# A single 512-wide scan per state group, and the inverse root of the variance as a power on GpSimd

## The reference

```python
def step(s, rkvw):
    r_t, k_t, v_t, w_t = rkvw
    a = k_t[..., :, None] * v_t[..., None, :]
    out = jnp.einsum('bhi,bhij->bhj', r_t, u * a + s)
    s = a + w_t[..., :, None] * s
    return (s, out)
```

```python
m = x.mean(-1, keepdims=True)
v = ((x - m) ** 2).mean(-1, keepdims=True)
(x - m) / jnp.sqrt(v + eps) * w + b
```

## Time and profile before

| | |
|---|---|
| time, 3 runs | 1427.91 us median (1426.55 to 1428.36) |
| the profiled execution, its own time | 1426.46 us |
| its span, first to last instruction | 1424.7 us |
| TensorE busy | 1272.8 us (89%) |
| VectorE busy | 978.7 us (69%) |
| ScalarE busy | 581.5 us (41%) |
| GpSimd busy | 563.7 us (40%) |
| mean granted TensorE clock | 0.976 |

### The profile page before, as it was taken

The page is one execution under the profiler, slowest core; times in us unless marked ns, Lnnn a source line. Parts: engine busy times, 40 slices in busy tenths (PEclk is TensorE's granted clock), DMA queues, the critical chain, the costliest instruction groups (busy, mean ns, idle before and its releaser), DMA issues. The chain is left out here.

```text
span 1424.7 us, 34363 instructions
## 1 busy us (share of the span) xinstructions
PE 1272.8 (89%) x12736; PEld 984.9 (69%) x12736; DVE 978.7 (69%) x1840; ACT 581.5 (41%) x1296; POOL 563.7 (40%) x512
## 2 busy tenths in 40 slices
PE   2999999699999889999977898988998898849798
PEld 2888888588888756667645666666666666627687
DVE  4677776566666611111113999999999999979787
ACT  2777776577777532221122222232222222213332
POOL 2877776477777510100002333333233333224111
PEclk9999999999999989999997999999999999979899
DMA  7200000111111000000000000000000000000011
GB/s 305 89 2 0 0 0 2 38 40 37 37 37 37 17 0 0 0 0 0 0 1 1 1 1 1 0 0 0 0 0 0 0 0 0 1 1 0 23 44 52
DMA packets 24922, 27.31 MB, mean 19 GB/s; under 512 B 2272, under 2 KB 20000, under 8 KB 23968
## 3 DMA queue, kind: packets, MB, share of 16 engines
q1 hardware_dynamic: 23568, 24.94, 5.1%
q10 hardware_dynamic: 1296, 1.58, 0.3%
HBM read 22.32 MB, written 4.19 MB: 19 GB/s over the span
## 5 line engine op out<-in xcount | busy, mean ns | idle before, releaser
L1167 DVE TENSOR_TENSOR_SCAN rec_st<-rec_wT,rec_st 128x256 f32<-128x256 f32 x256 | 202.7, 832 | 4.4
L681 DVE TENSOR_TENSOR x<-psum,x 128x256 f32 (+1 forms) x32 | 12.1, 420 | 203.7 <-PE psum L620 203.7
L803 POOL TENSOR_TENSOR rec_xm<-rec_mixed,rec_xa 128x512 f32<-128x512 f32 x80 | 94.3, 1179 | 141.1 <-DVE rec_mixed L1139 139.7
L944 PE MATMUL psum<-rec_vT,spread 128*128 128x256 f32 x512 | 140.0, 396 | 5.4 <-DVE rec_st L1159 4.7
L944 PEld LDWEIGHTS psum<-rec_vT,spread 128*128 128x128 f32 x512 | 88.7, 189 | 44.5 <-issue 21.9
L610 PE MATMUL psum<-gelu_lnT,w 128*128 128x512 f32 x256 | 113.9, 603 | 1.5 <-ACT gelu_lnT L642 1.5
L620 PE MATMUL psum<-w,gelu_hT 128*128 128x256 f32 x512 | 112.6, 381 | 0.8 <-ACT gelu_hT L651 0.8
L651 ACT ACTIVATE gelu_hT<-psum,cols 128x512 f32<-128x512 f32 x64 | 44.0, 687 | 161.3 <-PE psum L610 161.3
L620 PEld LDWEIGHTS psum<-w,gelu_hT 128*128 128x128 f32 x512 | 96.6, 190 | 15.9 <-ACT gelu_hT L651 1.6
L267 POOL TENSOR_TENSOR cross_z<-cross_z,cross_bias 128x512 f32<-128x512 f32 x64 | 80.3, 1278 | 54.2 <-DVE cross_z L498 54.2
L812 POOL TENSOR_TENSOR rec_st<-rec_st,rec_rT 128x512 f32<-128x512 f32 x32 | 40.7, 1272 | 150.3 <-DVE rec_st L1167 150.3
(11 more groups left out here) (173 smaller groups left out, 2908.5 us busy)
## 6 DMA issues: line engine op xcount, KB each, us to landing
cross_encT<-in_enc SPq DMA_DIRECT2D x64, 128.0 KB, 2.5
x<-in_x SPq DMA_DIRECT2D x4, 1024.0 KB, 9.2
out<-x SPq DMA_DIRECT2D x16, 256.0 KB, 2.0
w<-in_w SPq DMA_DIRECT2D x2, 1024.0 KB, 8.9
cross_mask<-in_cross_mask SPq DMA_DIRECT2D x1, 1024.0 KB, 4.7
w_qkv<-in_w_qkv ACTq DMA_DIRECT2D x1, 768.0 KB, 11.3
w_kv<-in_w_kv SPq DMA_DIRECT2D x1, 512.0 KB, 5.8
spread<-in_spread SPq DMA_DIRECT2D x1, 512.0 KB, 10.5
```

The lines of the kernel that those rows point to most:

```text
L803: nc.gpsimd.tensor_tensor(xm[:, m % 2, :, :].rearrange("p h (b t) -> p (h b) t", t=S), mixed[:, m % 2, :, :].rearrange("p h (b t) -> p (h ...
L944: last = nc.tensor.matmul(v_bank[:, jj * RT:(jj + 1) * RT], core.spread[:, half * JQ + jl, :], vT[:, u, jq, :], start=True, stop=True)
L1167: last = nc.vector.tensor_tensor_scan(states, decays, states, 0.0, ALU.mult, ALU.add)
```

## The change

Two edits, in different blocks.

In the recurrence, `wT` gets an axis for the two value columns of a group: the decays are written twice, so that they lie as a 512-wide row that matches the state tile. ScalarE writes them with two activations, one for each half, whose input is broadcast over that axis. VectorE then runs one scan of 512 where it ran two of 256. The zero slots are set in the larger tile.

In the norm phases the epsilon is added by VectorE, and GpSimd raises the sum to the power of -0.5 against a tile of constants -0.5. The root on ScalarE and the reciprocal on VectorE are gone.

```diff
@@ load_phase
             nc.gpsimd.memset(core.eps[:, :], EPS).then_inc(prepared, 1)
+            nc.gpsimd.memset(core.minus_half[:, :], -0.5).then_inc(prepared, 1)
...
@@ norm_phase
             nc.vector.scalar_tensor_tensor(out=c, in0=a, scalar=1.0 / C, in1=b, op0=ALU.mult,
-                                           op1=ALU.add).then_inc(var_ready, 1)
-            dve.wait_ge(std_ready, 1)
-            nc.vector.reciprocal(core.rstd[:, :], a).then_inc(step, 1)
+                                           op1=ALU.add).then_inc(step, 1)
             dve.wait_ge(step, 4)
+            nc.vector.tensor_scalar(c, c, EPS, None, ALU.add).then_inc(var_ready, 1)
+            dve.wait_ge(rstd_ready, 1)
             nc.vector.scalar_tensor_tensor(out=core.neg_mean[:, :], in0=core.neg_mean[:, :], scalar=-0.5,
                                            in1=core.rstd[:, :], op0=ALU.mult, op1=ALU.mult)
 
-        @block.scalar
-        def _(act):
-            act.wait_ge(var_ready, 1)
-            nc.scalar.activation(a, c, ACT.Sqrt, bias=core.eps[:, :]).then_inc(std_ready, 1)
+        @block.gpsimd
+        def _(pool):
+            pool.wait_ge(var_ready, 1)
+            nc.gpsimd.tensor_tensor(core.rstd[:, :], c, core.minus_half[:, :], ALU.pow).then_inc(rstd_ready, 1)
@@ recurrence_phase
-        wT = sb("wT", [P, 2, HALVES * RB, S])
+        wT = sb("wT", [P, 2, HALVES, JG, RB, S])
...
-                nc.scalar.activation(wT[:, u, :, 1:S], decay_exp[:, :, 0:S - 1], ACT.Exp, scale=-1.0).then_inc(w_ready, 1)
+                for half in range(HALVES):
+                    last = nc.scalar.activation(
+                        wT[:, u, half, :, :, 1:S],
+                        decay_exp[:, half * RB:(half + 1) * RB, 0:S - 1].unsqueeze(1).to_broadcast([P, JG, RB, S - 1]),
+                        ACT.Exp, scale=-1.0)
+                last.then_inc(w_ready, 1)
...
-                decays = wT[:, u, half * RB:(half + 1) * RB, :].rearrange("p b t -> p (b t)")
-                for jj in range(JG):
-                    states = st[:, n, jj, :, :].rearrange("p b t -> p (b t)")
-                    last = nc.vector.tensor_tensor_scan(states, decays, states, 0.0, ALU.mult, ALU.add)
-                last.then_inc(scanned, 1)
+                states = st[:, n, :, :, :].rearrange("p j b t -> p (j b t)")
+                nc.vector.tensor_tensor_scan(states, wT[:, u, half, :, :, :].rearrange("p j b t -> p (j b t)"), states,
+                                             0.0, ALU.mult, ALU.add).then_inc(scanned, 1)
```

More of the change, by code:

```diff
@@ L105, in _ @@
             nc.gpsimd.memset(core.eps[:, :], EPS).then_inc(prepared, 1)
+            nc.gpsimd.memset(core.minus_half[:, :], -0.5).then_inc(prepared, 1)
             nc.gpsimd.memset(core.maa_w2b[:, :, :], 0.0).then_inc(prepared, 1)
             nc.gpsimd.memset(core.td_w2[:, :, :], 0.0).then_inc(prepared, 1)
-            pool.wait_ge(prepared, 3)
+            pool.wait_ge(prepared, 4)
             pool.wait_ge(core.ones_set, 1)
@@ L133, in norm_phase @@
     with ExitStack() as ctx:
-        step, var_ready, std_ready = semaphores(nc, ctx, f"{name}_step", f"{name}_var_ready", f"{name}_std_ready")
+        step, var_ready, rstd_ready = semaphores(nc, ctx, f"{name}_step", f"{name}_var_ready", f"{name}_rstd_ready")
         block = ctx.enter_context(nc.Block())
@@ L1229, in _ @@
             nc.vector.memset(mixer_b[:, :], 0.0).then_inc(mixer_cleared, 1)
-            nc.vector.memset(wT[:, :, :, 0], 0.0)
+            nc.vector.memset(wT[:, :, :, :, :, 0].rearrange("p u h j b -> p (u h j b)"), 0.0)
             for half in range(HALVES):
@@ L1610, in build @@
         core.eps = sb("eps", [P, 1])
+        core.minus_half = sb("minus_half", [P, TILES])
         core.psum = ctx.enter_context(nc.psum_tensor("psum", [P, 8 * 512], FP32))
```

## The result

The changed kernel took 1461.64 us (median of 4 executions, 1453.17 to 1464.73). The kernel before, timed beside it, took 1428.13 us (4 executions, 1426.55 to 1436.32). The ratio is 1.0213, with a 95% interval of 1.0152 to 1.0275: slower, by 33.5 us, where I forecast faster. The profiled execution of the changed kernel took 1464.68 us for itself, with a span of 1462.9. Two later executions far out of line, one of 2215 us in e11 and one of 3233 us of the kernel before beside e9 to e11, are left out of the ratios.

What follows compares the result with a forecast made beforehand. VectorE's own instruction list was taken to bound the recurrence, and a serial chain the norms. Scan -9.0, stall +1.3, first pair -0.9, loads and decays +0.2, norms +3.4 gave -5.0 us: 1422.5, range 1416 to 1438.

Steps and rivals of the forecast that it cites:

- X: Length of GpSimd's power instruction in each norm, guessed at 1.2 us, with 0.3 and 4.5 as ends.
- the term of the norm phases: Five norms, root and reciprocal replaced by GpSimd's power: +3.4 us in all with the power at 1.2 us.
- 0.51 + X: Each norm after the change, from start of variance step to start of last step: 0.51 us plus the power.
- 5X - 2.6: Net time the five norms add, in us; they were to gain 2.6 less five powers.
- forty to seventy passes: Upper guess for GpSimd's power in the norms, counted in passes of 32 elements: 3 to 4.5 us.
- the first rival: The norms' power costs what the scan gives and more, from X = 2.2 us; about 1436 at X = 4; chance 0.31.
- element by element: Tail of the first rival: GpSimd's power in the norms costs tens of us each; chance 0.06.
- 0.07 us a group: Recurrence: one scan of 512 instead of two of 256 saves this; 16 runs x 8 groups give 9.0 us.
- The predicted stall of 0.09: Recurrence, first scan of a run waits for GpSimd's r times k product; 15 x 0.09 = 1.3 us given back.
- second decay activation: ScalarE, recurrence: 0.5 us more a run, hidden in 0.98 idle with 0.48 left; uncovered in the first run, +0.5.
- my terms: Recurrence: scan -9.0, stall +1.3, first run's pair -0.9, decay activation +0.5, table load -1.28 us.
- The load behind the barrier: Self-attention's start: the table load now delays ScalarE's first activation, +0.95 us.

Runs made afterwards that it cites:

- e11: The kernel before with two plain sums of 1024 on GpSimd in norm1 alone, for which its last step waits; 1437.87 us, ratio 1.0047.
- e9: The changed kernel itself, unaltered, timed and profiled once more; 1451.98 us, ratio 1.0152 to the kernel before.
- e10: The changed kernel with a product by 0.7 for the norms' power, and powers of 1 to 128 elements on GpSimd in the load block; 1454.64 us.
- e3: The changed kernel with a product by 0.7 in place of the power on GpSimd; 1429.1 us, ratio 0.999.
- e1: The kernel before with only the scan edit, its norm phases as before; 1426.51 us, ratio 0.998.
- e7: The changed kernel with a product by 0.7 for the power and an unused root on ScalarE in each norm, restoring the table loads' places; 1429.38 us.
- e12: The kernel before, unchanged, for one more profile; 1436.2 us, one execution.
- e4: The changed kernel with ten needless products on TensorE beside every norm; 1448.04 us, ratio 1.0124.
- e2: The kernel before with only the norm edit, two scans of 256 per group; 1460.58 us, ratio 1.0197.
- e5: The changed kernel with, for the power, three plain sums and a product by 0.7 on GpSimd; 1452.88 us, ratio 1.0146.

## Why the prediction was wrong

**The sign, and most of the size: X.** The step that failed is the term of the norm phases, where I counted the power "as about fourteen passes of 32 elements at 2 ns, X = 0.3 + 0.9 = 1.2 us". It measured 5.44. No run shows fourteen passes, or any number of them. The formula around it was right: 0.51 + X gives 5.95 and the trace has 5.96; five norms by 5X - 2.6 give +24.6, and the stages have +24.7. With the right X the same sum ends at 1421.5 + 5 x 4.24 = 1442.7 on the profiled execution. The range, 1416 to 1438, ended far below the 1461.64 that was measured. Its upper end was X = 4.3 to 4.5 from "forty to seventy passes", a number that no row held up; e10 shows why it was too low: the cost is 159 ns an element beside 1.9 for an ordinary one, as much as some eighty ordinary passes and not fourteen. This is the first rival, at 0.31. Its tail, "element by element" at 0.06, has the form right, since the time goes by the number of elements, but its price of tens of us each was far too high.

The Trainium skill ("GPSIMD Engine Reference", Elementwise — side-by-side cycle accounting) gives about 2.6 cycles an element for a GpSimd operation of two tensors, and 4497 ns for one of 2048 elements; that is about 2.2 ns an element, an estimate from the page's figures. The product of e3 and the earlier trace rows have 1.9 ns an element, of that order; for the power a rule for ordinary operations of two tensors doesn't hold, and the measurement decides.

**The scan: half the gain.** VectorE's own list does set the time, as I read it: in the steady stretch of the changed kernel (830 to 1290 us) it waits 2.9 us for TensorE, against 1.5.

```profile
DVE rec_st L1165 <- PE psum L945: 2.9, 5, 1.2
```

But the saving, 0.07 us a group, is 0.045 to 0.05: undisturbed 1.22 to 1.23 us against 1.27 to 1.28, beside the mixing product 1.71 against 1.76. A run of the recurrence went from 31.05 to 30.65, so 0.4 us and not 0.47; in e1 thirteen of them saved 5.2 us. The predicted stall of 0.09 at the first scan of each run isn't there: it takes 1.22 to 1.24 us in e1. The timing was as forecast, for from the fourth run to the fourteenth it starts 0.04 us before to 0.12 after the end of GpSimd's product in the kernel before and 0.01 to 0.16 before it in e1. But a scan that starts 0.50 us before that end takes only 0.36 longer (second run of e1), and one that starts 0.32 before it only 0.17 (third run), so the wait ends some 0.15 us ahead of the end that the profile gives, and this slack I hadn't counted. The first scan of all takes 2.13 us instead of 2.77 in the changed kernel. But from the last step of norm4 to the first scan of the second run e1 takes the same 64.4 us as the kernel before: the first scan starts 0.9 us later there, 0.5 of it for the second decay activation. The end of the recurrence, from the first scan of the fifteenth run on, then gave back 2.3 us in e1, which has two stretches of 3.4 us at half clock there that the kernel before hasn't. That makes the recurrence 2.4 to 5.0 us shorter over the executions, where my terms come to 9.4.

**What was right.** The second decay activation is hidden: 0.98 us of idle time became 0.46, and 0.48 was forecast. The load behind the barrier costs 1.0 us (0.95 forecast), and ten loads became five. The one of the recurrence went into idle time, and the forecast gain of 1.28 us is there: from the last step of norm4 to the first scan it is 33.4 us in e1 and e7, with the load in its old place, and 32.1 in e3, with the clock at half for 20.5 us in all three. Of the other loads nothing shows in the whole time, where e3 and e7 both have a median of 1429 us. The scan's wait for a product of GpSimd on the same memory stayed at half a microsecond for a scan twice as long. That is as the Trainium skill ("SBUF — State Buffer", Who interferes with whom) has it, with one side excluded until the other's instruction ends.

**What wasn't in it at all: TensorE's clock.** The prediction put the clock at nothing, without a reason. Of the 1461.64 us, 1442.7 are the prediction with the right X. In e9, an execution without slow ends, it took 1451.1: 4.4 of the 8.4 more are the recurrence, 2.0 and 2.0 the starts of the two attention stages. The first profiled execution had two slow ends on top, 13.6 us with what else varies. Read from before's trace alone this was visible only in part: one profile and three times, all of the lower group.

The Trainium skill ("TensorE: Matmul & The Clock Gate", HAM oscillation — how this bites in real kernels) has the clock fall in the gaps between bursts of work and cost half the speed until it is back. The trace agrees behind the norms: TensorE was idle for 5.8 us around norm2 of the kernel before, and the clock was at 1.2 GHz (granted 0.50) for 6.8 us from 259.7. The slow starts and ends are less plain a case: the same 1.90 us of idle time had full clock behind it once and half clock once (e12), and with the norms' gap filled (e4) both attention stages still started slowly.

**What stays open.** What decides whether an attention stage starts or ends at half clock. The kernel before has a slow end, e7 has it with norms of 2.2 us, and e9 does not have it with norms of 7.4. Whether the change makes it more frequent isn't settled: all executions of e2 (norms 7.4, two scans) lie 5.9 us or more above the lowest of the changed kernel, of which the scan's gain explains no more than 5, and three of four of e5 are in its upper group. Of the profiled attention stages, 6 of 18 with the norm edit have a slow end and 1 of 10 without it. But e11 with norm1 alone couldn't tell. Nor is it shown that products in the norms prevent a fall that comes at the other end of the stage. So the loss is 24.7 us from the power, shown by e3, e5 and the trace; what the scan gave and what the slow starts took nearly cancel in e9 (24.6 us above the profile of before), and 0 to 13 us more vary from execution to execution.

## What to carry to other kernels

Before an elementwise operation goes to another engine in a chain where each step waits for the last, measure that operation on that engine at the width in question; counting passes of an ordinary one missed by a factor of four and a half. A power on GpSimd wasn't worth it on this critical path: it takes 0.16 us for each element of a partition, against 0.97 us for the whole root, reciprocal and their handovers. Even for one element (0.56 us, and 0.51 around it) it would gain nothing, by this estimate. Of one profile and three times ask whether they are all of one group: here the kernel before itself varies by some 10 us between its groups, twice what the wider scan gives the recurrence.

## What the runs showed of the hardware

- GpSimd's power takes about 0.4 us and 159 ns an element: 0.563 us for 1, 1.656 for 8, 5.427 for 32, 20.782 for 128. A product of 32 takes 0.251, a sum of 1024 takes 1.89.
- VectorE's scan takes 1.22 us for 512 elements where two of 256 in a row take 1.27, so joining two saves only 0.05. From 256 to 512 elements it grows by 2.2 ns an element, twice the 1.06 of an ordinary operation.
- The same kernel on the same chip has times in groups, 1424 to 1428.6, 1433 to 1437 and 1441, with a mean granted clock of 0.975 to 0.978 in the first and 0.958 to 0.969 in the others. The two profiled executions differ in a few short stretches at 1.2 GHz.
- The same idle time of TensorE, 1.90 us at the same place of the same kernel, was followed by full clock in one execution and by half clock in another.
- Moving a table load of 1.28 us from behind a wait for TensorE into idle time gave 1.3 us (e3 against e7).
